# Planning a layer norm tile by tile in a gated attention block

## The chip, the cores and the metric

The kernel runs on one core of one Trainium2 chip. Its time is the time on the device in microseconds (us). A core has TensorE (PE, with its weight loads shown as PEld), VectorE (DVE), ScalarE (ACT), GpSimd (POOL) and SyncE (SP, which issues the DMAs here). Each engine works through its own queue in order; semaphores hold them together.

## The reference

Eight sequences of 1024 rows and 512 channels pass through two blocks:

```python
x = x + tanh(g_xattn) * xattn(layernorm(x), ctx)     # 8 heads of 64, context of 384 channels
x = x + tanh(g_ffn) * ffn(layernorm(x))              # 16 heads of 32, normed queries, gated output
# layernorm: (x - mean) / sqrt(var + 1e-5) over the 512 channels
# attention, both times: softmax(q k^T * scale) v, then an output projection;
# the second one scales each output row by a sum of top-3 gates
```

## The kernel before, in words

There are 16 stages, j = 0 to 15: stages 0 to 7 are the first block on each sequence, 8 to 15 the second block. A stage has 64 steps (T); in a step PE makes the scores of 128 keys against 512 queries for each head of a group (2 heads in the first block, 4 in the second), ACT takes the exponentials (`ex`), PE multiplies them with the values (`PV`), and POOL adds them up (`ad`) for the softmax sum. POOL adds in six or seven of each eight steps. PE also makes, for the next group of heads, the scores once more for their maxima (`mx`), and DVE reduces each 128x1024 of them (`mxr`, L1281); after eight such tiles of a head, `mt` and `ml` turn the maxima into a row and a DMA (`md`) puts it in place.

While stage j - 1 runs, the input of stage j is prepared in two halves of 512 rows, n = 0 and 1, each of four tiles of 128 rows by 512 channels in the buffer `xs`. For a half:
- `xl`: the DMA brings four tiles into `xs`.
- `ln` on DVE: four `bn_stats` (L1226, one for each tile), four `bn_aggr` (L1229), and one small instruction that adds the epsilon (L1231).
- `la` on ACT: Ln and Exp of four numbers per row (L1027, L1028).
- `lb` on DVE: four small instructions (L1235, two Newton steps at L1176 and L1177, L1238).
- `l2` on ACT: four scalings of a tile (L1035).
- `tr` on PE: transposes of the four tiles (L859), each followed by `tra` on ACT (L1042) and `trl` on DVE (L1245).

The order of every queue is made when the program is built. A list scheduler (`Plan.run`) gives each item an engine, a planned time, a due step and what it must come after; when an engine is free in its planned time, it takes the ready item with the lowest due step. Nothing interrupts an item, and all that an item holds is issued in one piece. The due steps of the first halves are 10 (first block) and 8 (second block) after the start of stage j - 1, those of the second halves 28.5 and 29. The values of the running stage (`vp` on PE, `vpe` on ACT at L1094 in the first block and on DVE at L1274 in the second) are due from step 0 on, exponentials at their own step less one, maxima of a group within its first 3 to 12 steps (first block) or 0.4 to 9.4 steps (second block). POOL's adds are at L817; DVE's lower half of the split attention output (`hsl`) is at L1297. In the waits of the trace, L902 is PE's `mx`, L911 its `mt`, L925 its scores and L942 its `PV`.

Of the kernel before, what the change touches and what calls it, by code (L numbers as in the profile page):

```python
# [15 lines left out]
ACT = mybir.ActivationFunctionType  # L16
# [103 lines left out]
def stage(j):  # L120
# [4 lines left out]
BATCH_HAS = {kind: n for n, kinds in (  # L125
    (1, ("xl", "cx", "cxl", "ln", "la", "lb", "l2", "tr", "tra", "trl", "wv", "wo", "xr")), (2, ("gm",)),
    (NG, ("wl", "pq", "pk", "pqa", "pka", "pql", "pkl", "ss", "ssa", "s2", "s3", "s3p", "sd", "mx", "mxr", "mt", "ml", "md")),
# [9 lines left out]
class Plan:  # L137
# [139 lines left out]
    def load(self, j):  # L277
# [11 lines left out]
        for n in range(2):  # L289
            self.add(("xl", j, 2 + n), "sp", 0.7, b0 + at["load"][n], [("tr", j, 0, NG - 1)] if n else [("st", TT * (j - 1) - 1), ("tr", j - 1, 1, NG - 1)])  # L290
            b = b0 + at["norm"][n]
            self.add(("ln", j, n), "dve", 3.5, b, [("xl", j, 2 + n), ("l2", j - 1, 1)])
            self.add(("la", j, n), "act", 0.5, b + 0.1, [("ln", j, n)])
            self.add(("lb", j, n), "dve", 0.8, b + 0.2, [("la", j, n)])
            self.add(("l2", j, n), "act", 3.2, b + 0.3, [("lb", j, n)])
            b = b0 + at["turned"][n]
            for k in range(NG):
                self.add(("tr", j, n, k), "pe", 0.5, b + k, [("l2", j, n)] + used)
                self.add(("tra", j, n, k), "act", 0.6, b + k, [("tr", j, n, k)])
                self.add(("trl", j, n, k), "dve", 0.7, b + k, [("tra", j, n, k)] + [("trl", j, n, k - 1)] * (k > 0))  # L300
# [152 lines left out]
def attention(nc, x, x1, out, ctxT, weights, w_split, small):  # L453
# [4 lines left out]
    with ExitStack() as ctx:  # L458
# [99 lines left out]
        ctx_hi_ok, ctx_lo_ok = sem("ctx_hi_ok"), sem("ctx_lo_ok")  # L558
        normed = sem("normed")
        norm_in = sem("norm_in")  # L560
# [42 lines left out]
        with nc.Block() as block:  # L603
# [222 lines left out]
            def _(pe):  # L826
# [23 lines left out]
                for it in sched:  # L850
                    kind, ph = it[0], stage(batch(it))
                    ffn, D, G = ph.ffn, ph.D, ph.G
                    if kind == "tr":
                        _, j, n, k = it

                        pe.wait_ge(normed, l2_at["l2", j, n])
                        out = bank(it)
# [118 lines left out]
            def _(act):  # L976
# [15 lines left out]
                for it in sched:  # L992
# [36 lines left out]
                    elif kind == "l2":  # L1029
                        _, j, n = it  # L1030

                        act.wait_ge(norm_in, 2 * j + n + 1)
                        for t in range(TT // 2):
                            i = n * TT // 2 + t
                            ins = act.activation(xs[:, t, :], xs[:, t, :], ACT.Identity, scale=rs[:, 1, i:i + 1], bias=rs[:, 0, i:i + 1])  # L1035
                        ins.then_inc(normed, 1)
                    elif kind == "tra":
# [124 lines left out]
            def _(dve):  # L1162
# [16 lines left out]
                for it in sched:  # L1179
# [33 lines left out]
                    elif kind == "fb":  # L1213
                        dve.wait_ge(f_in, 48)
                        link(dve.memset(blk[:], 0.0))
                        for e in range(F.G):
                            dve.memset(blk[e * F.D:(e + 1) * F.D, e * F.D:(e + 1) * F.D], 1.0)
                        dve.tensor_scalar(bo_f[:], bo_f[:], tg[:, 1:2], None, ALU.mult).then_inc(f_ok, 1)
                    elif kind in ("ln", "lb"):
                        _, j, n = it  # L1220
                        tiles = range(TT // 2)
                        r = slice(n * TT // 2, (n + 1) * TT // 2)
                        if kind == "ln":
                            dve.wait_ge(xs_loaded[2 + n], 16 * (j + 1))
                            for t in tiles:
                                ins = dve.bn_stats(st[:, r.start + t, :], xs[:, t, :])  # L1226
                            link(ins)
                            for t in tiles:
                                ins = dve.bn_aggr(mv[:, r.start + t, :], st[:, r.start + t, :])  # L1229
                            link(ins)  # L1230
                            dve.scalar_tensor_tensor(rs[:, 0, r], mv[:, r, 1], EPS, mv[:, r, 1], ALU.add, ALU.max).then_inc(rstd_in, 1)  # L1231
                            continue
# [155 lines left out]
```

## Time and profile before

| | us |
|---|---|
| median of 3 runs | 5170.55 |
| lowest and highest | 5155.74, 5205.7 |
| the profiled execution | 5195.86 |
| its span, first to last instruction | 5194.1 |
| PE busy | 4795.6 |
| POOL busy | 3366.2 |
| DVE busy | 3068.5 |
| ACT busy | 2597.6 |

The profile is of one execution; 1.8 us of its time lie outside its span. A busy PE is not a PE at its peak, since its clock has two levels; the clock granted to it is shown as a share of full speed, and its mean over the span was 0.965.

### The profile page before, as it was taken

What the parts mean: (1) busy time and instruction counts of PE and PEld (TensorE: products, weight loads), DVE (VectorE), ACT (ScalarE), POOL (GpSimd) and SP (SyncE); (2) the same over time, 40 slices, a digit from 0 to 9 for tenths busy, and PEclk for the clock granted to TensorE, in tenths of its full rate; (3) what the DMA queues carried; (4) which work ended last, traced back from release to release, by engine and by line L of the source; (5) the groups of instructions that cost most, each with busy time, mean ns of one, the idle gap of its engine ahead of it and who ended that gap; (6) DMA issues with size and microseconds to landing.
All of it is one profiled execution on the core that took longest, in us unless ns stands there. A gap on an engine that the chain in (4) does not pass through costs nothing.

```text
span 5194.1 us, 67121 instructions
## 1 busy us (share of the span) xinstructions
PE 4795.6 (92%) x21696; PEld 2744.4 (53%) x21696; DVE 3068.5 (59%) x3762; ACT 2597.6 (50%) x4673; POOL 3366.2 (65%) x2667
## 2 busy tenths in 40 slices
PE   4999999999999999998998998998998989989998
PEld 3555555555555556564564554554654644645644
DVE  4555545464646464566666756657656666667663
ACT  2444434353434443545646646546555456456364
POOL 1655656474656474747857857777588487578587
PEclk8999999999999999999999999999999999999998
DMA  7343434344343433432233132322323322322320
GB/s 233 94 133 105 123 106 119 114 118 130 86 138 86 127 97 107 98 101 72 67 98 74 44 110 60 82 82 64 93 64 74 90 64 60 90 76 56 98 50 25
DMA packets 285207, 481.08 MB, mean 93 GB/s; under 512 B 32832, under 2 KB 165440, under 8 KB 275648
## 3 DMA queue, kind: packets, MB, share of 16 engines
q1 hardware_dynamic: 284864, 476.79, 33.7%
q8 instruction: 181, 2.97, 0.2%
q14 instruction: 162, 1.33, 0.1%
HBM read 223.14 MB, written 50.33 MB: 53 GB/s over the span
## 4 chain that ended last, share of the span: by engine, by line
PE 48%; DVE 6%; issue 4%; ACT 2%; POOL 1%; SPq 1%; DMA 0%; ACTq 0%; POOLq 0%; DVEq 0%
PE aux L839 15%; PE acc L942 10%; PE aux L902 9%; PE scores L925 8%; DVE nm L1281 3%; PE aux L954 2%; PE aux L963 1%; DVE rs L1231 1%; PE aux L883 1%; POOL added_f L817 1%; PE aux L859 1%; SPq L734 1%; ACT probs L1127 0%; DMA stack<-ck_lo 0%; ACT xs L1035 0%
## 5 line engine op out<-in xcount | busy, mean ns | idle before, releaser
L1281 DVE TENSOR_REDUCE nm<-aux 128x1 f32<-128x1024 f32 x1536 | 1844.6, 1221 | 1203.3 <-PE aux L902 1200.8
L817 POOL TENSOR_TENSOR added<-added,probs 128x512 f32<-128x512 f32 x1433 | 1804.7, 1296 | 973.6 <-PE acc L942 696.6
L1127 ACT ACTIVATE probs<-scores 128x512 f32<-128x512 f32 x2151 | 1189.7, 597 | 880.7 <-PE scores L925 841.6
L925 PE MATMUL scores<-stack 128*128 128x512 f32 x4096 | 1351.3, 420 | 96.4 <-ACT probs L1127 53.6
L902 PE MATMUL aux<-stack 96*128 96x512 f32 (+1 forms) x3072 | 1022.2, 422 | 114.5 <-DVE nm L1281 78.1
L925 PEld LDWEIGHTS scores<-stack 128*128 128x128 f32 x4096 | 741.5, 191 | 708.8 <-issue 274.3
L942 PE MATMUL acc<-probs,vh 128*32 128x512 f32 (+1 forms) x4302 | 979.9, 623 | 60.7 <-ACT vh L1094 36.3
L902 PEld LDWEIGHTS aux<-stack 96*128 96x128 f32 (+1 forms) x3072 | 530.2, 191 | 597.2 <-DVE nm L1281 298.0
L817 POOL TENSOR_TENSOR added_f<-added_f,probs 128x512 f32<-128x512 f32 x537 | 678.9, 1299 | 59.2 <-PE acc L942 37.1
L839 PE MATMUL aux<-xT_hi,wqk 128*128 128x512 f32 x1536 | 579.8, 407 | 15.4 <-ACT qwork L1066 6.9
L1127 ACT ACTIVATE more<-scores 128x512 f32<-128x512 f32 x537 | 300.3, 598 | 184.0 <-PE scores L925 162.8
L839 PEld LDWEIGHTS aux<-xT_hi,wqk 128*128 128x128 f32 x1536 | 290.1, 189 | 113.4 <-issue 47.8
L804 POOL TENSOR_TENSOR cq_lo<-qwork,cq_hi 128x512 fp32r<-128x512 f32 x64 | 82.4, 1288 | 411.8 <-ACT cq_hi L1082 411.8
L942 PEld LDWEIGHTS acc<-probs,vh 128*32 128x32 f32 (+1 forms) x4302 | 158.0, 120 | 345.8 <-issue 236.8
L817 POOL TENSOR_TENSOR added_f<-added_f,more 128x512 f32<-128x512 f32 x231 | 294.8, 1304 | 33.3 <-PE acc L942 25.9
L817 POOL TENSOR_TENSOR added<-added,more 128x512 f32<-128x512 f32 x231 | 291.2, 1290 | 24.3 <-PE acc L942 23.7
L839 PE MATMUL aux<-xT_lo,wqk 128*128 128x512 f32 x768 | 302.2, 394 | 0.0
L942 PE MATMUL acc<-more,vh 128*32 128x512 f32 x1074 | 290.5, 620 | 0.0
L1304 DVE SCALAR_TENSOR_TENSOR aux<-aux,rn 128x512 f32<-128x512 f32 x128 | 88.8, 694 | 253.0 <-ACT rn L1140 238.2
L1127 ACT ACTIVATE added<-scores 128x512 f32<-128x512 f32 x256 | 143.5, 596 | 178.2 <-PE scores L925 174.6
L839 PE MATMUL aux<-wvo,halves_f 128*128 128x512 f32 x768 | 218.6, 427 | 1.5 <-issue 1.5
L823 POOL TENSOR_TENSOR xs<-xs,bo_x 128x512 f32<-128x512 f32 x64 | 81.8, 1292 | 163.2 <-DMA xs<-in_x 163.1
(130 smaller groups left out, 5057.9 us busy)
## 6 DMA issues: line engine op xcount, KB each, us to landing
wqk<-w_split SPq DMA_DIRECT2D x256, 256.0 KB, 3.8
wvo<-w_split SPq DMA_DIRECT2D x64, 1024.0 KB, 6.9
stack<-cq_hi SPq DMA_DIRECT2D x128, 256.0 KB, 5.0
stack<-ck_hi SPq DMA_DIRECT2D x128, 256.0 KB, 4.9
stack<-cq_hi SPq DMA_DIRECT2D x256, 128.0 KB, 2.4
stack<-ck_hi SPq DMA_DIRECT2D x256, 128.0 KB, 2.4
xs<-in_x SPq DMA_DIRECT2D x16, 1024.0 KB, 6.3
stack<-cq_lo SPq DMA_DIRECT2D x64, 256.0 KB, 4.8
```

The costliest lines, as they stand in the source:

```text
L734: sp.dma_start(stack[row:row + D, g % 2, e * ph.SLOTS + slot, :].bitcast(F32), src[what][half][e * D:(e + 1) * D, :].bitcast(F32)).then_in ...
L804: pool.tensor_tensor(cq["lo"][:, q], qy[:, n], cq["hi"][:, q].bitcast(F32), ALU.subtract).then_inc(qlo_ok, 1)
L817: pool.tensor_tensor(onto, onto, exp_buffer(T, e), ALU.add).then_inc(added_ok, 1)
L823: pool.tensor_tensor(xs[:, t % (TT // 2), :], xs[:, t % (TT // 2), :], bo[:], ALU.add).then_inc(biased, 1)
L839: ins = pe.matmul(out, lhs(a, k), rhs(c, k), start=k == 0 and i == 0, stop=k == whole - 1 and i == 2)
L902: ins = pe.matmul(aux[:, b + j, :], stack[used, g % 2, e * ph.SLOTS + qs, t * P:(t + 1) * P], stack[used, g % 2, e * ph.SLOTS + ks, j * HA ...
L925: ins = pe.matmul(scores[:, u % SCORES, :], stack[:, g % 2, e * ph.SLOTS + ks, jt * P:(jt + 1) * P], stack[:, g % 2, e * ph.SLOTS + qs, n ...
L942: ins = pe.matmul(acc[e * D:(e + 1) * D, :], v[:, g, jt * P + e * D:jt * P + (e + 1) * D], exp_buffer(T, e), start=jt == 0, stop=jt == TT - 1)
L954: ins = pe.matmul(out[e * D:(e + 1) * D, :], ones[:, 0:ph.SUM], exp_buffer(T, e), start=i == 0, stop=i == ph.APART)
L1127: act.activation(exp_buffer(T, e), scores[:, (n - 1) % SCORES, :], ACT.Exp, scale=ph.SCALE).then_inc(probs_ok, 1)
L1281: dve.tensor_reduce(nm[:, e * TT + t:e * TT + t + 1], keys, axis=AX.X, op=ALU.max, negate=True).then_inc(emptied["dve"], 1)
L1304: link(dve.scalar_tensor_tensor(src, src, -1.0, rn[:], ALU.mult, ALU.mult))
```

## The change

`ln` is cut: its four `bn_stats` become four items `bn` of 0.62 us each, and `ln` keeps the four `bn_aggr` and the small instruction, with a planned time of 0.7 us instead of 3.5. `l2` becomes four items of 0.78 us each instead of one of 3.2. All keep the due step of the item that they come from, and are chained one behind the other. Each `bn_stats` now raises a new semaphore `measured`, on which `ln` waits; each scaling raises `normed`, and PE waits for the fourth. The order of all queues is made anew with these items.

```diff
-            self.add(("ln", j, n), "dve", 3.5, b, [("xl", j, 2 + n), ("l2", j - 1, 1)])
+            for t in range(TT // 2):
+                self.add(("bn", j, n, t), "dve", 0.62, b, [("xl", j, 2 + n), ("bn", j, n, t - 1)])
+            self.add(("ln", j, n), "dve", 0.7, b, [("bn", j, n, TT // 2 - 1), ("l2", j - 1, 1, TT // 2 - 1)])
             self.add(("la", j, n), "act", 0.5, b + 0.1, [("ln", j, n)])
             self.add(("lb", j, n), "dve", 0.8, b + 0.2, [("la", j, n)])
-            self.add(("l2", j, n), "act", 3.2, b + 0.3, [("lb", j, n)])
+            for t in range(TT // 2):
+                self.add(("l2", j, n, t), "act", 0.78, b + 0.3, [("lb", j, n), ("l2", j, n, t - 1)])
             b = b0 + at["turned"][n]
             for k in range(NG):
-                self.add(("tr", j, n, k), "pe", 0.5, b + k, [("l2", j, n)] + used)
+                self.add(("tr", j, n, k), "pe", 0.5, b + k, [("l2", j, n, TT // 2 - 1)] + used)
...
-                        pe.wait_ge(normed, l2_at["l2", j, n])
+                        pe.wait_ge(normed, l2_at["l2", j, n, TT // 2 - 1])
...
-                        _, j, n = it
+                        _, j, n, t = it
+                        i = n * TT // 2 + t
 
                         act.wait_ge(norm_in, 2 * j + n + 1)
-                        for t in range(TT // 2):
-                            i = n * TT // 2 + t
-                            ins = act.activation(xs[:, t, :], xs[:, t, :], ACT.Identity, scale=rs[:, 1, i:i + 1], bias=rs[:, 0, i:i + 1])
-                        ins.then_inc(normed, 1)
+                        act.activation(xs[:, t, :], xs[:, t, :], ACT.Identity, scale=rs[:, 1, i:i + 1], bias=rs[:, 0, i:i + 1]).then_inc(normed, 1)
...
+                    elif kind == "bn":
+                        _, j, n, t = it
+                        dve.wait_ge(xs_loaded[2 + n], 16 * (j + 1))
+                        dve.bn_stats(st[:, n * TT // 2 + t, :], xs[:, t, :]).then_inc(measured, 1)
...
                         if kind == "ln":
-                            dve.wait_ge(xs_loaded[2 + n], 16 * (j + 1))
-                            for t in tiles:
-                                ins = dve.bn_stats(st[:, r.start + t, :], xs[:, t, :])
-                            link(ins)
+                            dve.wait_ge(measured, (2 * j + n + 1) * TT // 2)
```

## Rows read from the trace of the kernel before

**Rows 1.** The page: busy time of each engine over the span.

```profile
PE 4795.6 (92%) x21696; PEld 2744.4 (53%) x21696; DVE 3068.5 (59%) x3762; ACT 2597.6 (50%) x4673; POOL 3366.2 (65%) x2667
```

**Rows 2.** Groups of instructions by line, whole span: busy us, mean ns.

```profile
L1231 DVE SCALAR_TENSOR_TENSOR rs<-mv 128x4 f32<-128x4 f32 x32 | 116.2, 3631 | 1.1
...
L1297 DVE TENSOR_TENSOR halves_f<-vh,halves_f 128x512 fp32r<-128x512 f32 x64 | 86.6, 1373 | 9.6 <-ACT halves_f L1155 9.6
...
L1226 DVE BATCH_NORM_STATS2 st<-xs 128x6 f32<-128x512 f32 x128 | 79.0, 681 | 94.0 <-DMA xs<-in_x 74.0 <-DMA xs<-x_after_xattn 20.0
```

**Rows 3.** Waits from 2300 us on: us in total, times, longest us.

```profile
ACT rs L1027 <- DVE rs L1231: 85.2, 14, 8.9
...
PE aux L859 <- ACT xs L1035: 22.1, 7, 3.2
```

**Rows 4.** Timeline of DVE, second half of stage 15: start, us.

```profile
4648.88 2.46 DVE L1226 BATCH_NORM_STATS2 st<-xs 128x6 f32<-128x512 f32 x4
...
4651.79 8.30 DVE L1231 SCALAR_TENSOR_TENSOR rs<-mv 128x4 f32<-128x4 f32 x1
4660.01 2.34 DVE L1281 TENSOR_REDUCE nm<-aux 128x1 f32<-128x1024 f32 x2
4662.28 0.15 DVE L1235 TENSOR_TENSOR rs<-rs 128x4 f32<-128x4 f32 x1
```

**Rows 5.** Timeline of POOL, the same stretch.

```profile
4647.77 6.21 POOL L817 TENSOR_TENSOR added_f<-added_f,probs 128x512 f32<-128x512 f32 x5
...
4657.60 2.47 POOL L817 TENSOR_TENSOR added_f<-added_f,probs 128x512 f32<-128x512 f32 x2
```

**Rows 6.** Timeline of ACT, the same stretch; idle time before, in brackets.

```profile
4660.12 0.21 ACT L1027 ACTIVATE rs<-rs 128x4 f32<-128x4 f32 x1 [8.63 <-DVE rs L1231]
4660.36 0.21 ACT L1028 ACTIVATE rs<-rs 128x4 f32<-128x4 f32 x1
...
4663.05 2.93 ACT L1035 ACTIVATE xs<-xs,rs 128x512 f32<-128x512 f32 x4 [2.00 <-DVE rs L1238]
```

**Rows 7.** Timeline of PE, the same stretch.

```profile
4661.20 0.77 PE L925 MATMUL scores<-stack 128*128 128x512 f32 x1 [8.22 <-ACT probs L1127]
...
4666.03 1.33 PE L859 MATMUL aux<-ident,xs 128*128 128x128 f32 x5 [3.15 <-ACT xs L1035]
```

**Rows 8.** Busy us of PE, PEld, DVE, ACT, POOL by stretch, then PE's granted clock.

```profile
4660.10:4663.00 2.90, 1.14 (x2) 0.37 (x2) 2.80 (x7) 0.90 (x3) 0.00 (x0) 0.50 0.00 0
...
4666.00:4671.00 5.00, 4.97 (x24) 2.70 (x28) 0.69 (x1) 3.21 (x7) 0.00 (x0) 0.62 0.88 199
```

**Rows 9.** Timeline of DVE, first half of stage 3.

```profile
675.05 1.23 DVE L1231 SCALAR_TENSOR_TENSOR rs<-mv 128x4 f32<-128x4 f32 x1
676.86 0.64 DVE L1235 TENSOR_TENSOR rs<-rs 128x4 f32<-128x4 f32 x1 [0.58 <-ACT rs L1028]
...
680.01 1.20 DVE L1238 SCALAR_TENSOR_TENSOR rs<-mv,rs 128x4 f32<-128x4 f32 x1
```

**Rows 10.** Timeline of ACT, first half of stage 3.

```profile
681.25 2.93 ACT L1035 ACTIVATE xs<-xs,rs 128x512 f32<-128x512 f32 x4 [4.00 <-DVE rs L1238]
684.08 0.57 ACT L1094 ACTIVATE vh<-aux 128x512 f32<-128x512 f32 x1
```

**Rows 11.** Timeline of PE, first half of stage 3.

```profile
684.80 1.98 PE L942 MATMUL acc<-probs,vh 128*64 128x512 f32 x4 [4.05 <-ACT vh L1094]
```

**Rows 12.** Timeline of all engines, first half of stage 15.

```profile
4515.66 0.16 DVE L1231 SCALAR_TENSOR_TENSOR rs<-mv 128x4 f32<-128x4 f32 x1
4515.74 1.29 DVE L1274 TENSOR_TENSOR vh<-aux,bv 128x512 f32<-128x512 f32 x2
...
4517.77 2.52 POOL L817 TENSOR_TENSOR added<-added,probs 128x512 f32<-128x512 f32 x2 [4.30 <-PE acc L942]
```

**Rows 13.** Timeline of PE, second half of stage 3.

```profile
793.20 1.98 PE L942 MATMUL acc<-probs,vh 128*64 128x512 f32 x4 [4.82 <-ACT probs L1127]
```

**Rows 14.** The transposes (L859) between 600 and 900 us: first and last start.

```profile
L859 PEld LDWEIGHTS aux<-ident,xs x32: 138/140/143, 767.8 to 812.5; 128*128 128x128 f32 x32
```

More of the change, by code:

```diff
@@ L125 @@
 BATCH_HAS = {kind: n for n, kinds in (
-    (1, ("xl", "cx", "cxl", "ln", "la", "lb", "l2", "tr", "tra", "trl", "wv", "wo", "xr")), (2, ("gm",)),
+    (1, ("xl", "cx", "cxl", "bn", "ln", "la", "lb", "l2", "tr", "tra", "trl", "wv", "wo", "xr")), (2, ("gm",)),
     (NG, ("wl", "pq", "pk", "pqa", "pka", "pql", "pkl", "ss", "ssa", "s2", "s3", "s3p", "sd", "mx", "mxr", "mt", "ml", "md")),
@@ L558, in attention @@
         ctx_hi_ok, ctx_lo_ok = sem("ctx_hi_ok"), sem("ctx_lo_ok")
-        normed = sem("normed")
+        measured, normed = sem("measured"), sem("normed")
         norm_in = sem("norm_in")
```

## The prediction

> **What bounds the kernel now.** I read the page first. PE is busy 92% of the span, and no other engine more than 65% [rows 1], so a microsecond counts only where PE waits. The layer norm itself is small: 128 `bn_stats` are 79.0 us of DVE [rows 2]. But the next view, the groups by line, has an odd row: L1231, an instruction on four numbers per row, is busy 116.2 us for 32 instructions, 3.6 us each [rows 2]. It does nothing in that time; it waits. The waits from 2300 us on (stages 9 to 15 are prepared there, two halves each) say who pays: ACT stands 85.2 us behind it, and PE's transposes wait 22.1 us, in 7 places, for the scalings [rows 3].
>
> The timeline shows one such place; the second halves of stages 9 to 15 all look like it. DVE starts L1231 at 4651.79 and ends it 8.30 us later [rows 4]. POOL is in a run of adds that ends at 4657.60 + 2.47 = 4660.07 [rows 5], and L1231 ends at 4660.09. So the small instruction gets through when POOL's run is over. ACT waits 8.63 us for it with `la` at its head and all exponentials behind [rows 6], and PE is idle for 8.22 us for want of exponentials. Then two reductions of maxima (2.34 us) stand between L1231 and `lb` [rows 4], the scalings take 2.93 us [rows 6], and the transposes wait another 3.15 us [rows 7]. In all PE loses 8.22 + 3.15 = 11.4 us. After it stood for 8.22 us its granted clock is at 0.50 of full speed, the 1.2 GHz level, from 4660.1 to 4663, and 0.62 on average from 4666 to 4671 [rows 8].
>
> In the first block the second halves cost PE 4.82 us in a place such as stage 3 [rows 13]. There the first halves cost too: L1231 and the four instructions of `lb` each wait for one add (1.23 and 0.64 us for the first two, 1.20 for the last, the two between alike [rows 9], where 0.16 us is what L1231 takes alone [rows 12]), and PE waits 4.05 us for `vpe`, which stands behind the 2.93 us of scalings [rows 10, 11].
>
> **The change part by part.** No computing instruction is added or removed, and no DMA; the sum is of places. Profile and sum refer to 5195.86 us; the median of the runs is 25 us lower, and I carry the difference over to it unchanged.
>
> *Semaphores.* Each `bn_stats` and each scaling raises one more semaphore, 96 + 96 increments. The trace lets four `bn_stats` of 0.68 us pass in 2.46 us [rows 2, 4], so they overlap by (4 x 0.68 - 2.46) / 3 = 0.09 us. Cost: nothing at best; at worst the overlap is lost, 96 x 0.09 = 9 us of DVE, of which PE sees next to nothing since DVE is 59% busy. I take 0, since ACT's exponentials and DVE's reductions raise a semaphore each already and two reductions take 2.34 us here [rows 4]. (The Trainium skill, page "VectorE: DVE Perf Modes", section "The DRAIN you can't avoid", measured eight copies with a semaphore after each to be as long as with one at the end. No row here contradicts it.)
>
> *Second halves, second block (7 places, stages 9 to 15).* Here `bn` is due at step 29 and the last maxima of the group are due between 24 and 25.4, so wherever they become ready between two `bn` they go first. The two reductions that now follow L1231 [rows 4] are such: their 2.34 us move in front of it. POOL's run ends where it did, since the exponentials that it still adds were made before. So L1231 starts 2.34 us later and still ends at about 4660.1, with a wait of 6 us. `la` moves down ACT's order by as much, which lets some four exponentials, and PE's work behind them, into the idle stretch: 2.3 us. After the wait, `lb` can follow `la` at once, at 4660.57 + 0.13 = 4660.7 instead of 4662.28 [rows 4, 6]: 1.6 us. The scalings stay in one piece, as everything else ready on ACT is due later (exponentials at 30 and up), so the 3.15 us before the transposes stay. Per place 3.9 us, in seven 27 us. Bounds: 0, if the reductions are not ready between two `bn`; 7 x 11.4 = 80 us, if all of PE's loss goes. I take 27, as it is worked out from the rows of this very place. What is late next is L1231 itself, as before. The transposes, moved later by up to 2.3 us, are due at step 36.6, some 5 steps on.
>
> *Second halves, first block.* `bn` is due at 28.5, but the load of its tiles is itself due at 36.9 or follows the first half's transposes, so `bn` is overdue when it is ready, and all else that is ready on DVE and ACT is due later (maxima at 35, exponentials at 32 and up). The parts stay adjacent: 0. Bounds: the 4.82 us [rows 13] times seven, 34 us, gone or come again.
>
> *First halves, first block (7 places, stages 2 to 8).* The scalings are due at 10.3, while `vpe` and exponentials of steps 2 to 5 are ready; they slip in between scalings. `vpe` at 684.08 [rows 10] becomes ready within the 2.93 us and goes in half-way: 1.5 us of the 4.05 us [rows 11]. Gain 7 x 1.5 = 10 us, bounds 0 and 7 x 2.93 = 20 us. The last scaling comes later, which costs nothing: the transposes of that half begin at 767.8 [rows 14], 84 us on. The chain of five small instructions on DVE is untouched.
>
> *First halves, second block (7 places).* Two `vpe` of DVE, due at steps 0 and 1, now follow L1231 directly [rows 12]; with `bn` due at 8 one or both go in front of it. L1231 moves from 4515.66 by 0.65 or 1.29 us, and `lb`, which ended 0.1 us before POOL's run began at 4517.77 [rows 12], moves into that run. Each instruction of it then waits for an add as in rows 9, about 1.0 us. Between none and four of them: 0 to 4 us each place, and ACT waits with exponentials behind. I take one, 7 x 1.2 = 8 us lost, since `vpe` earlier also means `PV` earlier and the shift is only a part of an add.
>
> *All else.* `ln` and `bn` together are planned at 3.18 us instead of 3.5, `l2` at 3.12 instead of 3.2, so the order of all later items can shift by a place. The nearest price is L1297, which also has two inputs in the same memory: 86.6 us for 64 [rows 2], where undisturbed ones would take 64 x 0.68 = 44. Such waits can vanish (-43 us) or come again. I take 0 and keep 43 us for both ends.
>
> Sum: -27 - 10 + 8 = -29 us. From 5195.86 that gives 5167, from the median 5142.
>
> **The rivals.**
> 1. *The pieces stay together.* Items take the same places as before wherever nothing more urgent is ready between two pieces. This holds for a quarter of the halves by the due steps, and for all if the maxima and `vpe` become ready a little later than I think. Then 5170. For it: no row shows when the reductions' inputs were ready in the plan.
> 2. *L1231 waits for one add only.* Rows 9 show five waits of one add each in the middle of a POOL run of seven, rows 4 and 5 a wait through seven adds. If the place in the run decides and the second halves of the second block move into the first kind, PE gets 8.2 - 1.3 = 6.9 us back in each of 7 places, 48 us, with the 1.6 us for `lb`, 11 us, with -10 and +8 as above: -61, so 5110. Against it: they move deeper into the run, not towards its start. (The Trainium skill, page "SBUF — State Buffer", section "Who interferes with whom", has a rule for this: a DVE instruction with two SBUF inputs and a GpSimd instruction that reads SBUF exclude each other, and the second blocks until the first has finished. By that rule every wait would end with one add. Rows 9 agree, at 1.2 us; rows 4, at 8.30 us, do not, so the sum goes by the row.)
> 3. *The first halves of the second block fall into a POOL run, slower than before.* If more goes between their `bn` than one `vpe` and L1231 starts over 4517.77 - 4515.66 = 2.1 us later [rows 12], it meets the new run, and if it then waits as in rows 4 the price is 8.1 us for each of 7 places, 57 us, and to this comes the half clock after such a stop: PE was busy 1.14 and 4.97 us at 0.50 and 0.62 of full speed [rows 8], which is 0.6 + 1.9 = 2.5 us lost, 17 us in seven places. With the gains of 37 us: +37, so 5208; without them 5245. For it: those halves have three items of higher urgency near. Against: the one price seen so early in a run is one add.
>
> **How the numbers follow.** The forecast, 5142, has 0.48; rival 1 0.17, rival 2 0.15, rival 3 0.20. Within 1% (5119 to 5222) is about what a measurement of this kernel tells from no change: the three runs before lie 1% apart. Of the forecast's 0.48, with 43 us to each side, 0.13 are faster by over 1%, 0.32 within, 0.03 slower; of rival 1, 0.02, 0.14 and 0.01; of rival 2, 0.10 and 0.05; of rival 3, 0.08 within and 0.12 slower. Together 0.25, 0.59 and 0.16. The range goes down to rival 2 less half the 43 us, 5084, and up to half-way between rival 3 with and without the gains, 5227.
>
> **What would show it.** In the timeline of the second halves of stages 9 to 15 two reductions should stand before L1231's successor, its duration should be near 6 us instead of 8.3, and PE's idle time before the next score under 6.5 us. In the first halves of stages 2 to 8 `vpe` should stand between scalings, and PE's wait for it be under 3 us. L1231's group should be near 116 - 7 x 2.3 = 100 us. The prediction is wrong if that group falls by more than 50 us or rises (the waits have moved), or if L1297's changes by over 20 us.

## The result and the profile after

| | before | changed |
|---|---|---|
| median of 4 runs, us | 5174.28 | 5241.76 |
| lowest and highest | 5155.74, 5205.7 | 5222.04, 5262.79 |
| the profiled execution | 5195.86 | 5222.04 |

The changed kernel takes 1.0124 times as long, with an interval of 1.0089 to 1.0158: 1.2% slower, where 0.6% faster was forecast, and beyond the end of the range. A second set of runs on another chip gave 1.0111 (1.0082 to 1.0140). The profiled executions are only 26 us apart, because that of before lies 21.6 us above its own median and that of the changed kernel, its shortest run, 19.7 us below; so stretches of the trace are compared below, and the total is told by the ratios.

The page's busy times, against [rows 1]: PE 6.8 us more, DVE 13.8 us less.

```profile
PE 4802.4 (92%) x21696; PEld 2750.2 (53%) x21696; DVE 3054.7 (59%) x3762; ACT 2596.9 (50%) x4673; POOL 3366.2 (64%) x2667
```

The groups by line answer to [rows 2]. The small instruction (now L1233) fell from 116.2 to 94.0 us, the lower halves of the attention output (now L1299) from 86.6 to 68.7, and `bn_stats` (now L1223) rose by 1.8 us. By these groups alone one would expect a faster kernel.

```profile
L1233 DVE SCALAR_TENSOR_TENSOR rs<-mv 128x4 f32<-128x4 f32 x32 | 94.0, 2937 | 1.1
L1299 DVE TENSOR_TENSOR halves_f<-vh,halves_f 128x512 fp32r<-128x512 f32 x64 | 68.7, 1092 | 8.8 <-ACT halves_f L1156 8.8
L1223 DVE BATCH_NORM_STATS2 st<-xs 128x6 f32<-128x512 f32 x128 | 80.8, 681 | 98.2 <-DMA xs<-in_x 76.7 <-DMA xs<-x_after_xattn 21.5
```

The waits from 2300 us on answer to [rows 3] (us in total, times, longest). The first is much as it was (85.2 us). In the second the transposes wait 70.8 us for the scalings instead of 22.1, since the stop that stood before the next scores now stands here (shown in the part on why the prediction was wrong). The third is new: PE's `PV` stands 25.6 us, in seven places, behind a `vpe` of DVE (L1276). The trace of before has no such line.

```profile
ACT rs L1030 <- DVE rs L1233: 90.8, 14, 8.4
...
PE aux L862 <- ACT xs L1037: 70.8, 7, 10.3
...
PE acc L945 <- DVE vh L1276: 25.6, 7, 4.2
```

The new wait lies in the first halves of the second block. This is DVE's timeline of that place in stage 15 (start, us), to be held against [rows 12]:

```profile
4538.95 1.29 DVE L1223 BATCH_NORM_STATS2 st<-xs 128x6 f32<-128x512 f32 x2 [2.11 <-DMA xs<-x_after_xattn]
4540.15 0.67 DVE L1276 TENSOR_TENSOR vh<-aux,bv 128x512 f32<-128x512 f32 x1
4540.74 1.28 DVE L1223 BATCH_NORM_STATS2 st<-xs 128x6 f32<-128x512 f32 x2
4542.05 0.38 DVE L1231 BATCH_NORM_AGGREGATE mv<-st 128x2 f32<-128x6 f32 x4
4542.47 1.00 DVE L1233 SCALAR_TENSOR_TENSOR rs<-mv 128x4 f32<-128x4 f32 x1
...
4544.06 0.66 DVE L1237 TENSOR_TENSOR rs<-rs 128x4 f32<-128x4 f32 x1
4544.75 1.19 DVE L1177 SCALAR_TENSOR_TENSOR rs<-rs 128x4 f32<-128x4 f32 x1
4545.98 1.19 DVE L1178 SCALAR_TENSOR_TENSOR rs<-rs 128x4 f32<-128x4 f32 x1
4547.19 1.18 DVE L1240 SCALAR_TENSOR_TENSOR rs<-mv,rs 128x4 f32<-128x4 f32 x1
4548.30 0.68 DVE L1276 TENSOR_TENSOR vh<-aux,bv 128x512 f32<-128x512 f32 x1
```

And POOL, then PE, in the same stretch:

```profile
4542.16 3.76 POOL L820 TENSOR_TENSOR added<-added,probs 128x512 f32<-128x512 f32 x3 [2.44 <-PE acc L945]
```

```profile
4549.13 1.07 PE L945 MATMUL acc<-probs,vh 128*32 128x512 f32 x3 [4.19 <-DVE vh L1276]
```

The same place of the kernel before began with this line:

```profile
4512.74 2.47 DVE L1226 BATCH_NORM_STATS2 st<-xs 128x6 f32<-128x512 f32 x4 [2.17 <-DMA xs<-x_after_xattn]
```

One `vpe` went in between the `bn_stats`. L1233 therefore no longer starts 2.1 us ahead of POOL's run but 0.3 us after its start. Only 0.6 us of this is its own delay: counted from the first `bn_stats`, it starts at 3.52 us instead of 2.92. The other 1.8 us are POOL's: its run starts at 3.21 us instead of 5.03 [rows 12], as it waits for `PV`, and `PV` starts sooner because a `vpe` came sooner. The trace has the same 3.52 and 3.21 us in each of stages 10 to 15; in stage 9 the small instruction still gets through in 0.16 us. So it and the four instructions of `lb` all wait for an add: 1.00, 0.66, 1.19, 1.19 and 1.18 us, where L1231 took 0.16 us and the first of `lb` 0.15 us when POOL was quiet [rows 4, 12]. The second `vpe`, which before stood directly behind L1231, now stands behind `lb`, and PE's next matmul needs it.

To size it, each stage is cut into eighths at ACT's copies of the attention result, one for each group of heads. The first two eighths of stages 9 to 14 (six stretches) hold the first half's layer norm, the fourth eighth of stages 8 to 14 (seven stretches) the second half's. The last line of the windows view gives the length and busy time of all stretches together. First the two first eighths, before and then changed:

```profile
sum 687.60, PE 658.48 PEld 407.87 DVE 394.23 ACT 322.52 POOL 366.69; mean PE 109.75 PEld 67.98 DVE 65.71 ACT 53.75 POOL 61.11
```

```profile
sum 743.70, PE 679.22 PEld 416.69 DVE 420.61 ACT 323.28 POOL 368.49; mean PE 113.20 PEld 69.45 DVE 70.10 ACT 53.88 POOL 61.42
```

They are 56.1 us longer, 9.4 us a stage. Of this, 35.4 us are idle time of PE (29.1 to 64.5), 5.9 us a stage, and for 20.7 us, 3.5 us a stage, PE is busy for longer with the same number of matmuls. The rows of single stretches show why; the columns are as in [rows 8], the granted clock third from the end. This is stage 11's stretch before and changed:

```profile
3357.40:3472.20 114.80, 110.18 (x521) 68.50 (x513) 65.69 (x102) 53.73 (x98) 61.25 (x50) 0.97 0.32 97
```

```profile
3369.60:3493.90 124.30, 114.04 (x521) 69.61 (x513) 70.12 (x102) 54.02 (x97) 62.03 (x50) 0.93 0.30 91
```

The clock averages 0.93 instead of 0.97. Right after the stop of stage 15 the row is this, where the stretches before and after it show 1.00:

```profile
4549.00:4553.00 4.00, 3.87 (x14) 1.88 (x15) 0.37 (x1) 3.79 (x7) 4.00 (x4) 0.58 0.00 0
```

Between the levels of 1.2 and 2.4 GHz that is the lower one for most of 4 us, after 4 us without a matmul. Now the fourth eighths, before and changed:

```profile
sum 336.00, PE 240.92 PEld 117.62 DVE 246.88 ACT 183.78 POOL 216.76; mean PE 34.42 PEld 16.80 DVE 35.27 ACT 26.25 POOL 30.97
```

```profile
sum 325.20, PE 234.89 PEld 115.94 DVE 229.25 ACT 183.69 POOL 216.79; mean PE 33.56 PEld 16.56 DVE 32.75 ACT 26.24 POOL 30.97
```

They are 10.8 us shorter, 6.0 us of it PE's busy time and 4.8 us its idle time. The whole first block, up to the copy that ends it, is as long as it was: 2252.2 us before, 2253.9 us changed, and 2251.7 us in the second profile of the changed kernel. So the two stretches together, +56.1 - 10.8 = +45 us, 0.9% of the span, carry most of the loss.

### The profile page after: what moved, and what is told of

It reads as the page before. It is cut to its first block, busy times and chain, and to the rows that moved or that the text cites. A ratio compares the mean times of both kernels' runs of the same rounds, so it can differ in the third digit from the quotient of the medians.

```text
span 5220.3 us, 67121 instructions
## 1 busy us (share of the span) xinstructions
PE 4802.4 (92%) x21696; PEld 2750.2 (53%) x21696; DVE 3054.7 (59%) x3762; ACT 2596.9 (50%) x4673; POOL 3366.2 (64%) x2667
## 3 DMA queue, kind: packets, MB, share of 16 engines
q14 instruction: 162, 1.33, 0.1%
## 4 chain that ended last, share of the span: by engine, by line
PE 46%; DVE 6%; issue 4%; DMA 2%; ACT 2%; POOL 1%; SPq 1%; ACTq 0%; POOLq 0%; DVEq 0%
PE aux L842 13%; PE acc L945 9%; PE aux L905 9%; PE scores L928 8%; DVE nm L1283 3%; PE aux L957 2%; PE aux L966 1%; DMA out<-xs 1%; PE aux L886 1%; POOL added_f L820 1%; DVE rs L1233 1%; DMA xs<-x_after_xattn 1%; PE aux L862 1%; DVE st L1223 1%; ACT probs L1128 1%
## 5 line engine op out<-in xcount | busy, mean ns | idle before, releaser
L928 PEld LDWEIGHTS scores<-stack 128*128 128x128 f32 x4096 | 737.2, 191 | 653.2 <-issue 228.8
L842 PE MATMUL aux<-xT_hi,wqk 128*128 128x512 f32 x1536 | 581.0, 408 | 21.5 <-DMA wqk<-w_split 9.6
L820 POOL TENSOR_TENSOR added<-added,more 128x512 f32<-128x512 f32 x231 | 290.6, 1285 | 24.1 <-PE acc L945 21.5
L1306 DVE SCALAR_TENSOR_TENSOR aux<-aux,rn 128x512 f32<-128x512 f32 x128 | 88.8, 694 | 260.7 <-ACT rn L1141 254.3
L842 PE MATMUL aux<-wvo,halves_x 128*128 128x512 f32 x768 | 188.9, 397 | 0.4 <-DVE nm L1283 0.4
```

What stands on the lines that cost most here:

```text
L820: pool.tensor_tensor(onto, onto, exp_buffer(T, e), ALU.add).then_inc(added_ok, 1)
L842: ins = pe.matmul(out, lhs(a, k), rhs(c, k), start=k == 0 and i == 0, stop=k == whole - 1 and i == 2)
L928: ins = pe.matmul(scores[:, u % SCORES, :], stack[:, g % 2, e * ph.SLOTS + ks, jt * P:(jt + 1) * P], stack[:, g % 2, e * ph.SLOTS + qs, n ...
L1306: link(dve.scalar_tensor_tensor(src, src, -1.0, rn[:], ALU.mult, ALU.mult))
```

## The experiments

Ratios are to the kernel before, timed on the same chip. "First" and "fourth" are the changes of the two sums above against before, +56.1 and -10.8 us for the changed kernel.

**Each half of the change alone.** The first kernel cuts only the measuring:

```diff
-            self.add(("ln", j, n), "dve", 3.5, b, ...)
+            for t in range(TT // 2):
+                self.add(("bn", j, n, t), "dve", 0.62, b, ...)
+            self.add(("ln", j, n), "dve", 0.7, b, ...)
             self.add(("l2", j, n), "act", 3.2, b + 0.3, [("lb", j, n)])
```

> Only bn_stats is cut into four items, the scalings stay one item. Theory 1 (the loss comes from the first halves of stages 10 to 15, where one vpe now stands between bn_stats and the rest of the chain falls into POOL's run of adds): as slow as the changed kernel, 1.010 to 1.016 of before, with PE's wait of 4.2 us for DVE's vpe in each of those stages. Rival A (the cut of the scalings or the added semaphores cost it): 0.995 to 1.005. Rival B (the number of long waits at the attention output's lower half, L1297, differs by chance between the kernels): anything, with the per-stage lengths equal once those waits are taken off.

Measured: 1.0072 (1.0047 to 1.0097), first +50.3 us, fourth -10.6 us. That is less than I expected, with the place as expected. PE's new wait is there, as large as in the changed kernel:

```profile
PE acc L944 <- DVE vh L1277: 25.6, 7, 4.2
```

The second cuts only the scaling:

```diff
             self.add(("ln", j, n), "dve", 3.5, b, ...)
-            self.add(("l2", j, n), "act", 3.2, b + 0.3, [("lb", j, n)])
+            for t in range(TT // 2):
+                self.add(("l2", j, n, t), "act", 0.78, b + 0.3, [("lb", j, n), ("l2", j, n, t - 1)])
```

> Only the scalings are cut into four items. Theory 1: 0.995 to 1.005 of before; the items of ACT stay adjacent nearly everywhere, and the order of DVE is that of before. Rival A (scalings and semaphores): 1.010 to 1.016. The pure gain that the prediction gave to the first halves of the first block (10 us) should show here as 0.998 at most; in the changed kernel's trace vpe did not go between the scalings of stage 3, so I expect none of it.

Measured: 1.0004 (0.9985 to 1.0023), first -0.7 us, fourth -1.7 us. The loss of these two kernels belongs to the cut of the measuring. Cutting the scaling alone gives neither a loss nor a gain that the runs can tell.

**The order alone, with nothing cut.** The kernel before, with `ln` told to come after the first `vpe`, and the second `vpe` after `lb`, in the first halves of the second block:

```diff
-            self.add(("ln", j, n), "dve", 3.5, b, [("xl", j, 2 + n), ("l2", j - 1, 1)])
+            self.add(("ln", j, n), "dve", 3.5, b, [("xl", j, 2 + n), ("l2", j - 1, 1)] + [("vpe", TT * (j - 1))] * (j > B and n == 0))
...
-                ... + freed + ([("fb", 0)] if ph.ffn else []))
+                ... + freed + ([("fb", 0)] if ph.ffn else []) + [("lb", j + 1, 0)] * (ph.ffn and t == 1))
```

> The kernel before, with nothing cut; in the first halves of the second block ln comes after the first vpe and the second vpe after lb, as in the changed kernel. Theory 1a: the wait of 4 us for vpe appears, and the time is 1.006 to 1.012 of before (some 40 to 60 us). Rival A2 and any theory that needs the cut itself: 0.998 to 1.003.

Measured: 1.0074 (1.0048 to 1.0101), first +40.2 us, fourth -0.7 us:

```profile
sum 727.80, PE 671.75 PEld 409.99 DVE 418.91 ACT 323.30 POOL 367.43; mean PE 111.96 PEld 68.33 DVE 69.82 ACT 53.88 POOL 61.24
```

```profile
PE acc L942 <- DVE vh L1274: 20.2, 7, 3.1
```

No item is cut and no semaphore added, and most of the loss comes all the same: 40.2 of the 56.1 us of the first eighths. That part is the order. POOL's run comes sooner here too, 2.57 us after the first `bn_stats` in stages 10 to 12.

**The order taken back, with everything cut.** The changed kernel, with the measuring of those seven halves made most urgent once its first tile is measured, so that nothing gets between:

```diff
-                self.add(("bn", j, n, t), "dve", 0.62, b, ...)
-            self.add(("ln", j, n), "dve", 0.7, b, ...)
+                first = 1000 * (ph.ffn and n == 0 and t > 0)
+                self.add(("bn", j, n, t), "dve", 0.62, b - first, ...)
+            self.add(("ln", j, n), "dve", 0.7, b - 1000 * (ph.ffn and n == 0), ...)
```

> The changed kernel, but in the first halves of the second block the four bn_stats and ln get a due step so low that nothing goes between them. Theory 1: no 4.2 us wait for vpe, the stretch from one accumulator copy to the next at the start of stages 9 to 14 back from 96 to 85 us, and with the 1 to 2 us per stage gained in the second halves 0.995 to 1.000 of before. Rival B: still 1.01.

Measured: 1.0004 (0.9986 to 1.0023), fourth -15.5 us, and first +19.3 us:

```profile
sum 706.90, PE 663.75 PEld 407.62 DVE 393.81 ACT 323.94 POOL 366.13; mean PE 110.63 PEld 67.94 DVE 65.63 ACT 53.99 POOL 61.02
```

The loss is gone, at the upper end of what I expected, and DVE's busy time in these stretches is back at 394 us. PE's wait for `vpe` is no longer in the trace. The 19 us that stay are not from `lb`: the trace shows maxima, a `vpe` and score matmuls in another order than before, and PE waits there for exponentials and for `nm`. That this order is the cause is my reading; no run has it alone.

The next kernel keeps the `vpe` between the `bn_stats` but puts `lb` back behind the second `vpe`:

```diff
-            self.add(("lb", j, n), "dve", 0.8, b + 0.2, [("la", j, n)])
+            self.add(("lb", j, n), "dve", 0.8, b + 0.2, [("la", j, n)] + [("vpe", TT * (j - 1) + 1)] * (j > B and n == 0))
```

> The changed kernel, but in the first halves of the second block the four small instructions of lb come after the second vpe, as they did before the change; bn_stats stay cut, with a vpe between them. Theory 1a (the loss comes from vpe standing behind small instructions that wait for POOL): PE's wait of 4.2 us goes, the first two eighths of stages 10 to 14 take 115 to 117 us instead of 124, 1.000 to 1.003 of before. Rival A2 (the loss comes from the later start of the whole chain, since one vpe stands between bn_stats): as the changed kernel, 1.008 to 1.012.

Measured: 1.0029 (1.0008 to 1.0050), first +24.0 us, fourth -13.6 us, as expected. PE's wait is nearly gone:

```profile
PE acc L945 <- DVE vh L1276: 1.9, 6, 0.3
```

DVE is busy 416.7 us there, as in the changed kernel (420.6): the small instructions still wait in POOL's run. With the same waits but nobody behind them, 32 of the 56 us are gone. What costs is thus less the waiting of `lb` than the `vpe` queued behind it.

**What the small instructions wait for.** The changed kernel, with the five small instructions reading one tensor each:

```diff
-                            dve.scalar_tensor_tensor(rs[:, 0, r], mv[:, r, 1], EPS, mv[:, r, 1], ALU.add, ALU.max).then_inc(rstd_in, 1)
+                            dve.tensor_scalar(rs[:, 0, r], mv[:, r, 1], EPS, 0.0, ALU.add, ALU.max).then_inc(rstd_in, 1)
```

(and the other four alike).

> The changed kernel with its order, but the small instruction of ln and the four of lb read one tensor from SBUF instead of two. This leaves out the Newton step of the reciprocal root and the product of mean and root. Theory 1 in its part on the port (an instruction with two SBUF inputs waits for POOL's adds): the group of the small instruction falls from some 100 us to 32 x 0.16 = 5 us, the 8 us stops of the second halves and the 1.2 us waits go, and the time falls by 16 halves x 5 to 8 us plus the first halves' 4 us, in all 100 to 150 us: 0.98 to 0.99 of before. If a one-input instruction waits as well, nothing changes: 1.012.

Measured: 1.0082 (1.0051 to 1.0113). My expectation fell: with one input they wait as long as with two.

```profile
L1233 DVE TENSOR_SCALAR rs<-mv 128x4 f32<-128x4 f32 x32 | 99.1, 3096 | 1.1
```

(The Trainium skill, page "SBUF — State Buffer", section "Who interferes with whom", lists `tensor_scalar` among the operations that, with fitting operands, can take the pair of ports that DVE shares with GpSimd, and says that `tensor_reduce` never does. This row and those of the next run agree.)

So the same kernel with reductions over one element in their place:

```diff
-                            dve.scalar_tensor_tensor(rs[:, 0, r], mv[:, r, 1], EPS, mv[:, r, 1], ALU.add, ALU.max).then_inc(rstd_in, 1)
+                            dve.tensor_reduce(rs[:, 0, r], mv[:, r, 1:2], axis=AX.X, op=ALU.max).then_inc(rstd_in, 1)
```

> The changed kernel with its order, but the small instruction of ln and the four of lb are reductions over one element, which read one tensor. This leaves out the epsilon, the Newton step and the product of mean and root. Theory 1b (the small instructions wait for a port that POOL's adds hold, and bn_stats, bn_aggr and reductions do not use it): the group of the small instruction falls from 94 us to 32 x 0.16 = 5 us, the 8 us stops and the 4 us waits for vpe go, and the time is 0.975 to 0.985 of before. Rival D (any instruction at this place waits, whatever it reads): 1.008 to 1.012, with the group near 94 us.

Measured: 0.9762 (0.9737 to 0.9786), first +9.5 us, fourth -50.7 us, as theory 1b had it.

```profile
L1233 DVE TENSOR_REDUCE rs<-mv 128x4 f32<-128x4 f32 x32 | 5.0, 157 | 1.1
```

An instruction of the same size, in the same queue, beside the same POOL runs: 0.157 us on average instead of 2.94. And the same reductions in the order of before:

> The kernel before with its order and nothing cut, and the five small instructions as reductions over one element, as in the reduction variant of the changed kernel (0.976). This leaves out the epsilon, the Newton step and the product of mean and root. Theory 1d (the change loses only through waits for POOL's adds): the two reduction variants are equal within 0.3%, or the cut one is ahead by up to 10 us, so 0.974 to 0.979. Rival (the cut itself costs): this one at 0.968 or less.

Measured: 0.9728 (0.9701 to 0.9756), first -8.2 us, fourth -61.2 us. This is the price of all the waits of these small instructions in the kernel before: 2.7%. Of the 153.8 us by which its trace is shorter than before's, 86 fall in the first block. It also shows that with no such waits at all the cut order still comes out a little longer, by 0.9762 - 0.9728 = 0.3%, with intervals that overlap by 0.0019. They are of two chips, so the ratios are a hint and no more; it lies between what theory 1d and its rival had set. The stretches of the two traces say the same: those of the cut order are 17.7 us (first) and 10.5 us (fourth) longer. So some 18 to 19 of the changed kernel's +56.1 us come without the small instructions' waits, as in the kernel with the first halves whole.

**Moving the second halves' wait.** The kernel with the first halves kept whole, and the scheduler told that `la` is ready 6 us (5 us in the first block) after `ln` in the second halves, so that ACT isn't held:

```diff
+def j_ffn(it):
+
+    return it[1] > B
...
-                    events.append((now + time + self.LANDING.get(it[0], self.LAG[name]), None, it))
+                    late = {"ln": 6 if j_ffn(it) else 5}.get(it[0], 0) if it[0] == "ln" and it[2] == 1 else 0
+                    events.append((now + time + self.LANDING.get(it[0], self.LAG[name]) + late, None, it))
```

> The variant whose first halves are left whole (1.000 of before), with one more edit: in the second halves the planner counts 6 us (second block) or 5 us (first block) from ln to la, so that ACT gets la some 7 to 8 exponentials later. Theory 1c (PE stops 8 us because la, which waits for ln, stands ahead of exponentials on ACT): VectorE's wait stays, PE's stop before the next scores falls from 8 to under 3 us in 7 stages and from 4.8 to under 1 us in 5, and the time is 0.985 to 0.992 of before. Rival E (exponentials need what DVE does behind the waiting instruction, or POOL never drains): 0.998 or more.

Measured: 0.9991 (0.9972 to 1.0010), where theory 1c had 0.985 to 0.992; rival E's range is met. In stage 12's second half, ACT waits 2.15 us for a small instruction that still takes 5.66 us, and the fourth eighths shrink from 336.0 to 228.8 us, with less work in them (162 matmuls each instead of 175). The end of the small instruction's wait, `la` and the scalings now lie behind the fourth eighth (stage 11's ends at 3551.0 us), so this stretch alone says little about the gain.

```profile
3554.68 0.21 ACT L1037 ACTIVATE rs<-rs 128x4 f32<-128x4 f32 x1 [2.15 <-DVE rs L1240]
```

```profile
sum 228.80, PE 207.14 PEld 100.62 DVE 194.11 ACT 154.62 POOL 191.24; mean PE 29.59 PEld 14.38 DVE 27.73 ACT 22.09 POOL 27.32
```

The kernel as a whole is no faster. The fifth to eighth eighths of stages 9 to 14, before and in this kernel:

```profile
sum 968.20, PE 905.46 PEld 510.85 DVE 681.51 ACT 587.87 POOL 798.03; mean PE 150.91 PEld 85.14 DVE 113.59 ACT 97.98 POOL 133.01
```

```profile
sum 1027.00, PE 936.49 PEld 523.56 DVE 718.33 ACT 612.39 POOL 822.42; mean PE 156.08 PEld 87.26 DVE 119.72 ACT 102.07 POOL 137.07
```

58.8 us of the 107 come back there, 31.0 us of them PE being busy for longer, some of it with the matmuls that left the fourth eighth, and 27.8 us new idle time. The lower halves of the attention output (here L1306) also rose, from 86.6 to 101.3 us. The traces account for the rest: stage 8's last four eighths are 15.8 us longer (171.8 instead of 156.0), the first eighths of stages 9 to 14 9.5 us, and all else 5.1 us. So the trace is 18.0 us shorter than before's, which itself lies 19.2 us above the median of before on this chip. In PE's waits from 2300 us on, those for exponentials fell (behind `probs` from 47.9 to 21.5 us, behind `more` from 35.4 to 14.2), those for the scalings vanished (22.1), and those for DVE's `nm` (from 72.1 to 92.6 and from 18.4 to 31.8) and for the DMA of `ck_lo` (from 10.1 to 24.8) rose. So 69.7 us of waits went and 48.6 us came back as others.

**A version without the waits.** The chain of small instructions is moved to ACT: DVE ends the measuring with a reduction that writes the mean with its sign turned, and ACT does the rest, but for the Newton step, which is left out.

```diff
-            self.add(("lb", j, n), "dve", 0.8, b + 0.2, [("la", j, n)])
+            self.add(("lb", j, n), "act", 0.9, b + 0.2, [("la", j, n)])
...
+                            dve.tensor_reduce(rs[:, 0, r], mv[:, r, 0:1], axis=AX.X, op=ALU.max, negate=True).then_inc(rstd_in, 1)
...
+                        link(act.activation(rs[:, 1, r], mv[:, r, 1], ACT.Ln, bias=eps[:]))
...
+                            ins = act.activation(rs[:, 2, i:i + 1], rs[:, 0, i:i + 1], ACT.Identity, scale=rs[:, 1, i:i + 1])
```

First on the changed kernel, then on the kernel before:

> The changed kernel, with the small instructions taken off DVE: ln ends in a reduction that negates the mean, and ACT does Ln with the epsilon as bias, Exp, and four products of mean and root. This leaves out the Newton step; all else of the layer norm is computed. As far as theory 1b holds, no wait for POOL is left in the layer norm: 0.975 to 0.982, the four products costing ACT 32 x 0.8 us, of which PE sees under half.

> The kernel before, with the same move to ACT and nothing cut; it leaves out the Newton step. 0.975 to 0.984. Theory 1d: within 0.3% of the variant with the cut. Where the cut is worth what the prediction hoped, the cut one is ahead by 0.2 to 0.5%.

Measured: 0.9894 (0.9870 to 0.9917) on the changed kernel, 0.9887 (0.9860 to 0.9914) on that before, 5124.08 us. Both beat both kernels, by about half of the gain that I expected (0.975 to 0.982 and to 0.984), and the cut makes no difference between them that the runs can tell. In the trace of the second, the first block is 40 us shorter where the reductions gave 86, and the last four eighths of stages 8 to 14 are 34 us longer than before; why is open. ACT pays 27.2 us for 128 products of one number a row and DVE's last instruction takes 5.0 us in all; the lines are of the version on the kernel before:

```profile
L1036 ACT ACTIVATE rs<-rs 128x1 f32<-128x1 f32 x128 | 27.2, 283 | 0.9
...
L1240 DVE TENSOR_REDUCE rs<-mv 128x4 f32<-128x4 f32 x32 | 5.0, 157 | 1.1
```

**The changed kernel once more**, to size what the two stretches leave open.

> The changed kernel itself once more, beside runs of before on one chip, since the kernel with only bn_stats cut gave 1.0072 and the one with only the order changed 1.0074 where the changed kernel had given 1.0124 in four runs. Theory 1 (the same cause, and the rest is how often the 9 us waits at the attention output's lower half happen to fall): 1.007 to 1.010. If there is a second cause that needs both cuts: 1.011 to 1.014 again.

Measured: 1.0111 (1.0082 to 1.0140), first +52.5 us, fourth -12.3 us. In this trace the lower halves of the attention output are busy 83.1 us, about as in before's (86.6), and its time, 5234.8 us, is 38.9 us above before's profiled 5195.86. That fits +52.5 - 12.3 = +40.2 us. In the first trace of the changed kernel they were 68.7 us, 17.9 us less than before's, and it was only 26 us above. The ratio came out where I had put a second cause that needs both cuts (1.011 to 1.014); its interval covers the other range (1.007 to 1.010) as well, so this decides nothing.

## Why the prediction was wrong

Put side by side, the two stretches give the ratios of most kernels that leave the arithmetic alone. They fall short for the changed kernel, and the last line doesn't fit at all, since there the work and the waits moved to other stretches:

| | first + fourth, us | over 5194 us | measured |
|---|---|---|---|
| only the measuring cut | +50.3 - 10.6 | +0.76% | +0.72% |
| only the scaling cut | -0.7 - 1.7 | -0.05% | +0.04% |
| first halves whole | +19.3 - 15.5 | +0.07% | +0.04% |
| `lb` behind `vpe` | +24.0 - 13.6 | +0.20% | +0.29% |
| order alone | +40.2 - 0.7 | +0.76% | +0.74% |
| changed | +56.1 - 10.8 | +0.87% | +1.24% |
| changed, second time | +52.5 - 12.3 | +0.77% | +1.11% |
| `la` late | +9.5 - 107.2 | -1.88% | -0.09% |

*First halves, second block: the step that failed.* It had the place and the first link right, and the size and the way to PE wrong. The prediction said that one or both `vpe` go in front of L1231 and that `lb` moves into POOL's run; that is what happened. It priced one wait, 1.2 us a place and 8 us in all, with a bound of 4 us a place. Measured were 9.4 us a stage. Five things were missing from the term. It left the start of POOL's run where it was, at 4517.77 us; an earlier `vpe` brings `PV` and so the run forward by 1.8 us, three times the 0.6 us by which L1231 itself moved back, and L1231 falls into the run as well. All four instructions of `lb` wait, 4.3 us from the start of the first to the end of the last. What is queued behind them was not asked after: the second `vpe`, on which PE's `PV` depends, so the wait reaches PE whole, by 4.19 us; the prediction named exponentials on ACT instead. PE then runs at the lower clock: as many matmuls keep it busy 20.7 us longer, 3.5 us a stage. And the order of the maxima shifts, which is what I take the rest to be with the halves kept whole, 19.3 us or 3.2 a stage. These sizes overlap and don't add up; the whole is 5.9 us idle and 3.5 us busy a stage. Rival 3 had the sign and the right place, its condition was met (against POOL's run, L1231 starts 2.4 us later, where it asked for 2.1), and it had even a charge for the clock (2.5 us), but it tied this to a wait of 8.1 us in one instruction. Measured was a chain of five waits of one add each, with `vpe` behind. The lines ahead of the result would have told: [rows 12] show both `vpe` in front of `lb`, and [rows 9] show that a chain of five that meets a run waits five times.

*Second halves, second block.* Two reductions stand in front of the small instruction, which takes 5.63 us where 6 were forecast, and still ends with POOL's run:

```profile
4680.38 2.36 DVE L1283 TENSOR_REDUCE nm<-aux 128x1 f32<-128x1024 f32 x2
...
4685.16 5.63 DVE L1233 SCALAR_TENSOR_TENSOR rs<-mv 128x4 f32<-128x4 f32 x1
```

```profile
4688.29 2.48 POOL L820 TENSOR_TENSOR added_f<-added_f,probs 128x512 f32<-128x512 f32 x2
```

But `la` was to let four exponentials pass and let one. ACT stands 8.16 us instead of 8.63 [rows 6], and PE's loss is 1.37 + 10.08 = 11.45 us in place of 11.4:

```profile
4690.82 0.20 ACT L1030 ACTIVATE rs<-rs 128x4 f32<-128x4 f32 x1 [8.16 <-DVE rs L1233]
```

```profile
4682.88 0.27 PE L914 MATMUL aux<-ident,nm 128*8 128x128 f32 x1 [1.37 <-DVE nm L1283]
...
4695.13 1.97 PE L862 MATMUL aux<-ident,xs 128*128 128x128 f32 x8 [10.08 <-ACT xs L1037]
```

Of the forecast 27 us, 10.8 came in these stretches. That is about the part of `lb`: with no reductions behind L1233, the scalings start 1.33 us after `la` instead of 2.93 [rows 6], 1.6 us in each of seven places. The 2.3 us of exponentials in the idle stretch did not come. The error was to let ACT's queue follow DVE's delay in full; the planner counts the small instruction at 0.7 us, knows nothing of the 6, and orders `la` by that.

*First halves, first block.* Forecast -10 us, measured nothing that the runs can tell. In stage 3 the four scalings are still one piece, with `vpe` behind:

```profile
684.04 2.93 ACT L1037 ACTIVATE xs<-xs,rs 128x512 f32<-128x512 f32 x4 [3.98 <-DVE rs L1240]
...
686.87 0.58 ACT L1095 ACTIVATE vh<-aux 128x512 f32<-128x512 f32 x1
```

PE's wait is 2.56 us where it was 4.05 [rows 11], but nothing was gained: from one `PV` to the next it is 7.40 us, and it was 7.41. The matmuls between took longer, at a granted clock of 0.56 instead of 1.00, and the wait is shorter by that. A low due step of `vpe` doesn't put it between the scalings unless the plan has it ready in just those 3 us; in the changed kernel this happened in two of the seven first halves (stages 6 and 7). In the kernel with only the scaling cut it happened in all seven that the prediction named. There PE's waits for `vpe` in the first block fell from 36.3 to 31.5 us, half of the forecast gain, and at 1.0004 (0.9985 to 1.0023) the runs can't tell that from nothing. The nought for the *second halves of the first block* agrees with the first block's equal length.

*Semaphores* at nought: right. The kernel with the first halves whole has all 192 more increments and stands at 1.0004, and `bn_stats` as a group cost 1.8 us more of DVE.

*All else* at nought within 43 us: not contradicted, and not shown. L1297's group fell by 17.9 us from the trace of before to that of the changed kernel, and it moves by 14.4 us between two traces of the same kernel (68.7 and 83.1). So it is no test of the change, as the prediction had made it. It matters for the time, though. These are the last four eighths of stages 9 and 10 in the kernel before, the first with one wait of 10 us at L1297, the second without:

```profile
2834.10:2998.20 164.10, 151.45 (x778) 85.42 (x774) 116.39 (x134) 97.98 (x181) 132.85 (x106) 0.98 0.23 60
3203.00:3357.40 154.40, 149.34 (x778) 84.07 (x774) 107.92 (x134) 97.94 (x181) 132.90 (x106) 1.00 0.25 63
```

One such wait makes the stage 9.7 us longer. The traces have four before, two and four in the changed kernel, and two to six in the others; L1297 takes 0.68 us in most other places.

Neither of the prediction's signs of being wrong came: the small instruction's group fell by 22.2 us, not by 50, and L1297's by under 20. Both watch how long DVE is busy, and the loss lay in what PE waits for. (The lower end of its range, 5110 - 21.5, is 5088 and not 5084; nothing hangs on it.)

*What stays open.* The stretches give 0.8 to 0.9%, the runs 1.1 to 1.2%: 17 to 19 us more. They are in no other stretch of the traces. The first trace of the changed kernel is 26.2 us longer than that of before: +45.3 in the two kinds of stretches, -19.9 in the last four eighths of stages 8 to 14, where it has two long waits fewer, and +0.8 in all else. The second is 38.9 us longer: +40.2, +3.4 and -4.7. But the profiled execution of before lies 21.6 us above its median, so a typical run of before must be shorter somewhere than its trace; two fewer long waits of L1297 would do, but no trace of such a run is there. Cutting the scaling on top of the measuring (1.0072 to 1.0124 and 1.0111) isn't explained by what it does alone.

## What to carry to other kernels

Cutting an item of a planned queue in pieces changes no work and still moves everything behind it, since others get in between. Before doing so, look at what stands closely in front of another engine's run, and ask whether that run moves too, count every instruction that would fall into it, not one, and then ask who is next in the same queue and who waits for that one. Where small instructions wait for another engine's run, moving them to a third engine or to an operation that doesn't wait (here 1.1%, and up to 2.7% if all waits went) was worth more than any order of them that was tried.

## What the runs showed of the hardware

An instruction on four numbers a row can wait through the whole rest of a POOL run, 5.63 us here and 8.30 before, or through one add, about 1.2 us, in the same kernel. No run shows what decides. A `tensor_scalar` with one input in SBUF waits like one with two (3.10 us on average against 2.94), while a reduction over one element takes 0.157 us, 0.160 at most in 32. A DVE subtraction of 128x512 elements with both inputs in SBUF (L1297) takes 0.68 us in most places and up to 10 us in some, and a stage of before with one of the long ones is 9.7 us longer than one without (164.1 and 154.4 us). And in the first eighths 5.9 us more of idle PE a stage came with 3.5 us more of busy PE for the same number of matmuls, at a lower granted clock (0.93 instead of 0.97 in stage 11).
